# Fused attention and expert block in fp32: the softmax is normalised on the probabilities, before their transposes, instead of on the output

## The reference

```
xn  = layernorm(x)                                  # x: 16 x 512 x 256, fp32
q, k, v = split(xn @ wqkv.T)                        # 16 heads of 64
q, k = rope(rmsnorm(q) * q_norm_w), rope(rmsnorm(k) * k_norm_w)
p   = softmax(causal(q @ k.T / 8))                  # per batch and head, 512 x 512
att = (p @ v) @ wo.T
e   = argmax(xn @ gate_w.T)                         # one of 8 experts for each row
out = x + att + xn + xn @ expert_w[e].T
```

## Time and profile before

| | us |
|---|---|
| median of 3 runs | 2103.28 (2102.5 to 2106.65) |
| the profiled execution, its own time | 2101.06 |
| its span in the profile | 2098.9 |
| PE busy | 2028.5 |
| DVE busy | 1626.8 |
| ACT busy | 1507.9 |
| POOL busy | 1321.2 |

### The profile page before, as it was taken

One profiled execution on the slowest core, in us unless ns is written; L12 is line 12 of the kernel. 1 busy time (PEld: TensorE's weight loads), 2 busy tenths in 40 slices (PEclk: granted clock), 3 DMA queues, 4 the chain that ended last, 5 costly groups with the idle time before them and its releaser, 6 DMA issues.

```text
span 2098.9 us, 46876 instructions
## 1 busy us (share of the span) xinstructions
PE 2028.5 (97%) x16008; PEld 1731.9 (83%) x16008; DVE 1626.8 (78%) x3785; ACT 1507.9 (72%) x4693; POOL 1321.2 (63%) x1957
## 2 busy tenths in 40 slices
PE   4999999999999999999999999999999999999997
PEld 4778888888888888888888888888888888888785
DVE  6788877877878787787877878788777878778665
ACT  4677777777777777777777767777777777777664
POOL 5557665576565766567666666557656667655654
PEclk9999999999999999999999999999999999999999
DMA  5112111122211222102221132221222122211234
GB/s 197 56 41 79 46 48 60 44 74 72 85 47 37 93 69 67 61 29 89 71 77 46 34 99 67 67 61 44 73 73 75 47 77 67 70 58 44 84 101 149
DMA packets 84251, 145.71 MB, mean 69 GB/s; under 512 B 9776, under 2 KB 62896, under 8 KB 83888
## 3 DMA queue, kind: packets, MB, share of 16 engines
q1 hardware_dynamic: 77872, 125.93, 18.9%
q0 software_dynamic: 6144, 16.79, 2.7%
HBM read 102.05 MB, written 40.63 MB: 68 GB/s over the span
## 4 chain that ended last, share of the span: by engine, by line
PE 86%; DVE 9%; ACT 3%; issue 2%; DMA 1%; POOL 1%; POOLq 0%; DVEq 0%; SPq 0%; ACTq 0%
PE ps_g L676 35%; PE ps_g L770 13%; PE ps_g L779 13%; PE ps_s L759 12%; PE ps_g L738 5%; PE ps_g L787 3%; PE ps_s L752 2%; DVE neg_max L972 2%; ACT prob L572 1%; DVE qk_sin L958 1%; PE ps_g L703 1%; DVE qk_cos L958 1%; DVE ss L961 1%; PE ps_g L685 1%; DVE k_t L966 0%
## 5 line engine op out<-in xcount | busy, mean ns | idle before, releaser
L486 POOL TENSOR_TENSOR qk_rot<-qk_cos,qk_sin 128x128 f32<-128x128 f32 x1024 | 459.1, 475 | 621.4 <-DVE qk_sin L958 608.6
L676 PE MATMUL ps_g<-w_qkv,xn_t 128*128 128x384 f32 (+1 forms) x3072 | 610.8, 347 | 5.4 <-DVE k_t L966 2.8
L572 ACT ACTIVATE prob<-ps_s,neg_max 128x256 f32<-128x256 f32 (+3 forms) x1024 | 528.5, 539 | 78.9 <-DVE neg_max L972 77.2
L676 PEld LDWEIGHTS ps_g<-w_qkv,xn_t 128*128 128x128 f32 x3072 | 529.2, 189 | 54.7 <-DVE qk_sin L958 33.1
L558 ACT ACTIVATE qk_sq<-ps_g 128x256 f32<-128x256 f32 x512 | 197.4, 386 | 433.1 <-PE ps_g L676 403.5
L972 DVE TENSOR_REDUCE neg_max<-ps_s 128x2 f32<-128x512 f32 (+3 forms) x512 | 397.4, 817 | 115.0 <-PE ps_s L759 115.0
L492 POOL TENSOR_TENSOR rms_inv<-ss,neg_half 128x8 f32<-128x8 f32 x256 | 425.1, 1661 | 0.0
L580 ACT ACTIVATE prob_t<-ps_g 128x512 f32<-128x512 f32 (+2 forms) x768 | 366.9, 535 | 12.1 <-PE ps_g L770 11.4
L770 PE MATMUL ps_g<-ident,prob 128*128 128x128 f32 x2560 | 352.4, 277 | 14.3 <-ACT prob L572 14.3
L770 PEld LDWEIGHTS ps_g<-ident,prob 128*128 128x128 f32 x2560 | 288.2, 141 | 44.6 <-issue 21.8
L497 POOL TENSOR_TENSOR qk_rot<-qk_rot,rms_inv 128x256 f32<-128x256 f32 x512 | 306.3, 619 | 20.1
(11 more groups left out here) (98 smaller groups left out, 2312.9 us busy)
## 6 DMA issues: line engine op xcount, KB each, us to landing
w_tile<-w_dram SPq DMA_DIRECT2D x120, 512.0 KB, 3.5
x_rows_s<-x_dram SPq DMA_DIRECT2D x120, 128.0 KB, 2.1
y_dram<-y_rows_s SPq DMA_DIRECT2D x120, 128.0 KB
xin<-in_x SPq DMA_DIRECT2D x16, 512.0 KB, 4.2
out<-acc SPq DMA_DIRECT2D x15, 512.0 KB, 5.1
w_dram<-w_tile SPq DMA_DIRECT2D x8, 512.0 KB, 3.0
x_dram<-xn SPq DMA_DIRECT2D x2, 1920.0 KB, 16.3
y_back<-in_expert_t SPq DMA_DIRECT2D x8, 256.0 KB, 4.0
```

The source lines that it names most:

```text
L486: r = pool.tensor_tensor(rot[:, :, a, :], cos[:, :, a, :], sin[:, :, 1 - a, :], ALU.add)
L572: r = act.activation(prob[:, n % 2, h, 0:w], ps_s[n % 2][:, h, 0:w], ACT.Exp, bias=neg_max[:, i, h:h + 1], scale=1.0, accum_out=row_sum[:, ...
L676: r = pe.matmul(ps, lhs(a, c), rhs(b, c), start=(c == parts[0] and (a, b) == TERMS[0]), stop=(c == parts[-1] and (a, b) == TERMS[-1]))
```

## The change

The probabilities are multiplied by the inverse of their row sum in SBUF before they are transposed. DVE inverts the sums of items 0 and 1 together, and later of items 2 and 3 (`scale_probs(u, 0)` and `scale_probs(u, 2)`). It scales the wide items itself, one instruction for each head; GpSimd scales the narrow items, both heads in one instruction. `prob` has a place for each item of a unit instead of two buffers used in turn. The transposes of `row_inv`, the copy to `inv_t` and the multiplication into `o_n` are gone; ACT and DVE read the output straight from PSUM.

The transposes of the probabilities come later: those of items 0 and 1 after the projection of the same pass, those of items 2 and 3 in the next pass, u + 1, where PE starts with pt2 of the unit before. On DVE, `find_slots` and `split_weights` move ahead of the rope product of unit u + 1, which is ahead of the scaling; `row_stats`, `take_xt`, `normalise_x`, `choose` and `add_experts` stand between the projection and the second scaling; `row_max(u, 2)` and `row_max(u, 3)` are apart.

```diff
 # GpSimd
+            def scale_probs(u, k):
+                n, w = NT * u + k, width(k)
+                pool.wait_ge(s_inv, 2 * u + k // 2 + 1)
+                pool.tensor_tensor(prob[:, :, prob_at(k):prob_at(k) + w], prob[:, :, prob_at(k):prob_at(k) + w],
+                                   sum_inv[:, k, :].unsqueeze(2).to_broadcast([P, HEADS_OF_PAIR, w]), ALU.mult).then_inc(s_narrow, 1)
...
                     rotate(u + 1, 2)
+                if live(u):
+                    scale_probs(u, 0)
+                if live(u + 1):
                     rotate(u + 1, 3)
                     scale(u + 1, (2, 3)).then_inc(s_scaled, 1)
+                if live(u):
+                    scale_probs(u, 3)
 # ScalarE
-            def take_inverse(u):
...
             def take_o(u):
-                act.wait_ge(s_o_n, u + 1)
-                act.activation(o_t[:, 0, u % 4, :], o_n[:, :], ACT.Copy).then_inc(s_o_hi, 1)
+                act.wait_ge(s_o, u + 1)
+                act.activation(o_t[:, 0, u % 4, :], ps_g[g_bank(u + 1, "o")][:, :], ACT.Copy).then_inc(s_o_hi, 1)
 # TensorE
             def transpose_probs(u, k):
-                pe.wait_ge(s_prob, 2 * (n + 1))
+                pe.wait_ge(s_narrow if narrow(k) else s_wide, 2 * u + k // 2 + 1)
...
-            def transpose_inverse(u):
...
 # VectorE
-            def invert_sums(u):
...
-            def normalise_o(u):
...
+            def scale_probs(u, k0):
+                dve.wait_ge(s_prob, 2 * (NT * u + k0 + 2))
+                dve.reciprocal(sum_inv[:, k0:k0 + 2, :], row_sum[:, u % 2, k0:k0 + 2, :]).then_inc(s_inv, 1)
+                dve.wait_ge(s_inv, 2 * u + k0 // 2 + 1)
+                for k in (k0, k0 + 1):
+                    if not narrow(k):
+                        n, w = NT * u + k, width(k)
+                        for h in range(HEADS_OF_PAIR):
+                            r = dve.tensor_scalar(prob[:, h, prob_at(k):prob_at(k) + w], prob[:, h, prob_at(k):prob_at(k) + w], sum_inv[:, k, h:h + 1], None,
+                                                  ALU.mult)
+                        r.then_inc(s_wide, 1)
```

More of the change, by code:

```diff
@@ L135, in block_program @@
         k_t = sb("k_t", [P, 2, T], F32R)
-        prob = sb("prob", [P, 2, 2, T])
+        prob = sb("prob", [P, 2, sum(range(1, NT + 1)) * P])
         prob_t = sb("prob_t", [P, 2, NT, T])
@@ L140, in block_program @@
         sum_inv = sb("sum_inv", [P, NT, 2])
-        row_inv = sb("row_inv", [P, NT, 2, D])
-        inv_t = sb("inv_t", [P, T])
-        o_n = sb("o_n", [P, T])
         o_t = sb("o_t", [P, 2, 4, T], F32R)
@@ L279, in projection, with prob_at @@
             return divmod(u - 3, 2)
+        def prob_at(k):
+            return sum(width(n) for n in range(k))
         def narrow(k):
@@ L781, in values @@
                 r.then_inc(s_o, 1)
-            def transpose_inverse(u):
-                pe.wait_ge(s_inv, u + 1)
-                ps = bank(g_bank(u + 1, "inv"), (s_inv_t, u + 1))
-                for i in range(NT):
-                    r = pe.transpose(ps[:, tile(i)], row_inv[:, i, :, :].rearrange("p h d -> p (h d)"),
-                                     ident[:, :])
-                r.then_inc(s_inv_ps, 1)
             def unit(u):
                 tiles = sorted_tiles(u)
+                if live(u - 1):
+                    transpose_probs(u - 1, 2)
                 if live(u):
                     scores(u, 0)
+                if live(u - 1):
+                    transpose_probs(u - 1, 3)
                 if live(u + 1):
                     qkv(u + 1, 3)
+                if live(u - 1):
+                    values(u - 1)
                 for i in tiles[0:2]:
                     transpose_xs(u, i)
-                if live(u - 1):
-                    transpose_inverse(u - 1)
-                    values(u - 1)
+                if live(u):
+                    scores(u, 2)
+                if projection(u):
+                    project(u)
+                if turns_x(u):
+                    transpose_xn(batch_of(u) + 1)
                 if live(u):
                     transpose_probs(u, 0)
-                    transpose_probs(u, 1)
-                    scores(u, 2)
-                if turns_x(u):
-                    transpose_xn(batch_of(u) + 1)
-                if projection(u):
-                    project(u)
                 for i in tiles[0:1]:
@@ L820, in unit @@
                 if live(u + 2):
-                    qkv(u + 2, 0)
                     qkv(u + 2, 1)
@@ L1007, in unit @@
                     row_max(u, 1)
+                if 0 <= u < E:
+                    split_weights(u)
+                if slots_in(u) is not None:
+                    find_slots(slots_in(u))
                 if live(u + 1):
                     rope_products(u + 1, 3)
+                if live(u):
+                    scale_probs(u, 0)
+                    row_max(u, 2)
                 for i in tiles[0:2]:
                     take_xs(u, i)
-                if slots_in(u) is not None:
-                    find_slots(slots_in(u))
-                if live(u) and pair_of(u) == START_PAIR:
-                    start_rows(batch_of(u))
+                if live(u - 1):
+                    take_o(u - 1)
+                if live(u):
+                    row_max(u, 3)
+                if projection(u):
+                    take_projection(u)
+                if live(u) and batch_of(u) + 1 < B and pair_of(u) == STATS_PAIR:
+                    row_stats(batch_of(u) + 1)
+                if turns_x(u):
+                    take_xt(batch_of(u) + 1)
+                if live(u) and batch_of(u) + 1 < B and pair_of(u) == NORM_PAIR:
+                    normalise_x(batch_of(u) + 1)
                 if live(u + 1) and pair_of(u) == CHOOSE_PAIR:
                     choose(batch_of(u) + 1)
-                if live(u) and batch_of(u) + 1 < B and pair_of(u) == NORM_PAIR:
-                    normalise_x(batch_of(u) + 1)
-                if live(u - 1):
-                    normalise_o(u - 1)
-                if live(u):
-                    row_max(u, 2)
-                    row_max(u, 3)
-                if turns_x(u):
-                    take_xt(batch_of(u) + 1)
-                if 0 <= u < E:
-                    split_weights(u)
-                if projection(u):
-                    take_projection(u)
-                if live(u - 1):
-                    take_o(u - 1)
                 b = added_in(u)
@@ L1036, in unit @@
                         add_experts(b, rows)
-                if live(u) and batch_of(u) + 1 < B and pair_of(u) == STATS_PAIR:
-                    row_stats(batch_of(u) + 1)
+                if live(u):
+                    scale_probs(u, 2)
+                if live(u) and pair_of(u) == START_PAIR:
+                    start_rows(batch_of(u))
                 for i in tiles[2:3]:
```

87 lines of the change are left out of this document (37 added, 50 removed).

## The result

The changed kernel takes 2169.48 us (median of 4 runs, 2167.96 to 2170.14), beside 2102.89 (2101.91 to 2106.65) for the kernel before: a ratio of 1.031, 95% interval 1.029 to 1.033. It is 3.1% slower. I had forecast 2096, so both the sign and the range were wrong.

What follows compares the result with a forecast made beforehand. PE was taken to bound the kernel. The sum was 2101.1 + 1 - 5.2 - 3.1 + 2 = 2095.8, with 2.2 for the median 2098, taken as 2096 us because allowances leaned slow; range 2050 to 2138.

Steps and rivals of the forecast that it cites:

- What PE loses: On PE, the four row_inv transposes go: 0.52 us a unit, 15.59 to 15.07, 67 us over 128 units.
- The two sizes of the collision: In the scaling of items 0 and 1: 0.48 us for one DVE instruction, 1.10 for GpSimd's scaling of item 0.
- Then DVE holds until 6.46, GpSimd goes next: First scaling: DVE's first instruction finishes undisturbed at 6.46, GpSimd ends at 7.42, DVE's second follows at about 7.7.
- My own case: Main forecast: chain 0.1 to 0.3 us late in ordinary units, more in others; range 2078 to 2112, chance 0.42.
- my clock: Forecast's time within a unit, in us, zero at PE's start of pt2; keys and queries' transposes due at 11.04.
- the chain beside it: DVE and ACT up to the expert product: low part at about 9.65, PE due at 9.4, charged no extra delay.
- GpSimd's chain: Scaling, rotation, power and multiplications up to the transposes of keys and queries: ends 11.22 including 0.05 to PE, 0.18 after 11.04.
- GpSimd loses the collision twice: Rival: DVE's second instruction also goes first, scaling ends 0.45 later, 2141 us; chance 0.25 together with the slow tensor_scalar.
- Its point of decision: For the rival of a twice-lost collision: with the chain later than 11.04 + 0.52, each ordinary unit is slower than before.
- The other units: Per sixteen units: find_slots 2.4 us, four behind indirect DMAs 4.8, no expert tile 0.9, normalise_x with add_experts 0.5, xn transposes nothing.
- I take them as unchanged: First eight units, where split_weights also stands ahead of the scaling: no change in time claimed.
- The end: Last units: 5.2 us of waiting for DVE's rope product go, and 6 x 0.52; eight DMAs end 2 us later.

Runs made afterwards that it cites:

- the eleventh experiment: Changed kernel with a small memset on GpSimd between its wait for the inverted sums and its scaling multiplication, so it starts slightly later: ratio 1.024 to the kernel before.
- the first experiment: Changed kernel with all scaling and reciprocals left out, probabilities unnormalised, the new order kept: 2036.18 us, ratio 0.972 to the kernel before.
- the fifth experiment: Changed kernel with VectorE's scaling in the tensor_scalar form that also writes an accumulator, into an unused tile: ratio 1.004 to the kernel before.
- third experiment: Changed kernel with VectorE scaling all four items and GpSimd's scalings gone: ratio 0.993 to the kernel before.
- the sixth: Changed kernel with item 0 scaled on VectorE too, so GpSimd scales only item 3: ratio 1.005 to the kernel before.
- The twelfth experiment: Kernel before with its division left out and old transpose order kept, VectorE's low part of the output ahead of the maxima of items 2 and 3: ratio 0.988.

## Why the prediction was wrong

**What PE loses: right.** Floor 15.07 forecast, 15.14 measured; 67 us in all forecast, 58 measured. The reason was incomplete: without the new order the missing transposes give 1.2%, and 1.5% come with it (in the middle group 0.6% and 2.5%).

**The two sizes of the collision: right.** DVE's 0.48 (I took 0.48) and GpSimd's 1.04 (I took 1.10).

**Where the 73 us between 2096 and 2169 are.** Some 45 in units 16 to 111 (1567 us, before 1521; I had 1 more), 14 in the first sixteen, 12 in units 112 to 126.

**Two steps failed. The first** is "Then DVE holds until 6.46, GpSimd goes next". It was taken from the earlier trace rows, where DVE came into GpSimd's work and still was through first, and from start times 0.11 apart. In the changed kernel the starts are 0.04 apart in nearly every unit, and GpSimd wins: of the 256 pairs of both scalings, 242 start 0.04 apart, and all of these have a stretched DVE instruction, 1.37 us for 512 columns and 0.87 for 384. The 0.11 came from the hand-over of 0.15 in the earlier trace rows, which is 0.08 here (864.61 to 864.69). My own case was the eleventh experiment: GpSimd 1.10 - 0.14 = 0.96 behind DVE's first (measured 0.90), keys and queries used at 11.22 on my clock (measured 850.56 - 839.24 = 11.32), so 0.28 late instead of 0.18. That experiment is still 2.4% slower than the kernel before. So the order of winning explains little of the miss; the larger error is the next one.

**The second, and the larger, is that the chain beside it was put at nothing.** I wrote "about 9.65, where PE is due at 9.4. This is the same shift, not one more." By these numbers it is 0.25 late, and I charged an ordinary unit 0.18. The due time was right (in the first experiment the product starts at 812.58 - 803.15 = 9.43). DVE is through with the first scaling at 7.96 instead of 7.7, its low part ends at 868.41 - 858.64 = 9.77, and PE starts 0.15 after that, where I had allowed 0.04. PE's delay of 0.49 is set by DVE alone. In the whole run PE waits 54.6 us for the low part (41.4, 10.7 and 2.5), in the first experiment 3.8. With the form of the fifth experiment, which leaves all work in place and takes the collision away, the ordinary unit is 15.15.

GpSimd's chain ends at 869.80 - 858.64 = 11.16, and with 0.05 to PE at 11.21, where I had 11.22. That is luck: the scaling ended 0.33 earlier than forecast, and the two additions behind it, which meet DVE's second instruction, took 0.36 longer. The rival "GpSimd loses the collision twice" had the right size of loss in an ordinary unit, by the opposite mechanism: GpSimd wins, and DVE pays. Its point of decision held: from 11.04 + 0.52 = 11.56 on an ordinary unit is slower than before, and the keys and queries are used at 870.22 - 858.64 = 11.58 (15.63 us, before 15.59).

**The other units were under-sized.** The changed kernel's group less the first experiment's is 15.6 us; I had 10.2. By units, measured and then forecast: seven ordinary ones 3.6 (1.6 for nine); the one with `find_slots` 2.1 (2.4; in most other groups 3.3 to 3.7, with a stretch at the lower clock, and less in the next unit, so that the groups are equal within 1 us); the four behind indirect DMAs, one of them the one without an expert tile, 1.2, 2.0, 1.6 and 1.6, together 6.4 (4.8 and 0.9; my 4.9 for four DMAs should have read 4 x (0.98 + 0.29) = 5.1); one with `choose` 1.4 and one with `add_experts` 1.4 (0.5 for a unit with `normalise_x` and `add_experts`; I had `choose` hidden); the two with transposes of xn 0.7 (nothing). So `find_slots` and the DMAs were about right, and ordinary units and DVE's other work were not.

**"I take them as unchanged" was wrong** for the first units: the first sixteen take 269.0 us instead of 255.4. With VectorE alone they take 258.3, and with `split_weights` late as well 252.1.

**The end** was to lose 5.2 us of waiting for DVE's rope product; PE's waits for it are now 10.1, at another place (the qkv product). Units 112 to 126 take 258.6 us instead of 252.7.

**The sum.** Against the kernel before, in shares of its time: four transposes less -1.2%, new order -1.5%, VectorE scaling +2.0% (third experiment), GpSimd in place of VectorE for the narrow items +3.9%. That they add up to the measured 3.1% proves nothing, since each is the step from one ratio to the next. Of the 3.9, 2.7 go with the collision (fifth experiment); the sixth has 1.2 with item 3 alone, from waiting for the sums ahead of the DMAs. In the third the ordinary unit is at the floor; its 2.0% are in units with extra work on DVE, which is busy for 225 of 249 us, and 13 us of the 42 in the first sixteen (258.3 instead of 244.9). The Trainium skill, page "SBUF — State Buffer", section "Who interferes with whom", says that the form which also writes out its accumulator stays off the shared port, and that of two others the one that issues first has it whole. The fifth experiment agrees with the first half (0.74 beside 1.04, unstretched). The second half doesn't match the recorded starts: with 0.04 between them the later one had the port. Whether the true issue is earlier than the record of GpSimd's start, or DVE asks for the port later than it starts, no run here tells.

The twelfth experiment's base differs from the changed kernel in more than order (places of the low part's copies), so it isn't shown that the 1.5% are the order's alone; the wait of 0.22 in 128 units would be 28 us, 1.3%.

## What to carry to other kernels

Before giving GpSimd a share of work on SBUF that VectorE does at the same moment, ask what both pay if they meet: here 1.04 us of help made VectorE's 0.48 into 1.37, and the kernel in which VectorE does all is 3.7% faster (0.993 / 1.031). When two engines are let go by the same instruction, work out both orders of winning, follow both chains to PE, the one that seems second too, and charge the later of the two, in the units with extra work as well. And leave out the new work in one run: it tells at once whether a loss lies in the order or in the work.

## What the runs showed of the hardware

- Starts 0.04 us apart, GpSimd later: VectorE's tensor_scalar waits for GpSimd's end and needs 0.28 more, 0.20 less than its 0.48. Starts 0.09 apart: GpSimd's multiplication waits, and needs 0.90 after VectorE's end, 0.14 less than its 1.04. So the start-up of the one that waits, or a part of it, runs beside the other's work.
- GpSimd's power on 128x8, 1.65 us, leaves VectorE's tensor_scalar alone: 469 to 486 ns for 512 columns inside it (third experiment).
- After the same wait of 2.0 us on TensorE its clock fell to 0.5 for 3.4 us in some units and not in others; where it did, the unit was 1.6 us longer (sixth experiment).
- tensor_scalar in SBUF with a scalar per row, fp32: 480, 419, 351 and 282 ns in the median for 512, 384, 256 and 128 columns when VectorE does all the scaling (the means of 398 and 291 for the last two hold some that met GpSimd's other work, up to 665); with an accumulator 744 and 611 ns for 512 and 384, and 83 for reading it.
- GpSimd's multiplication by an operand spread over the columns: 1.04 us for 512 columns, 0.61 for 256.
